# Group norm, gating and attention for 16 images on one core: the next image's statistics moved earlier, GpSimd's gating of x spread over 26 units

## The reference

```
# x: (16, 32, 32, 512) float32, that is 16 images of 1024 tokens x 512 channels
xn  = silu(group_norm(x, 32 groups) * scale + offset)     # per image, groups of 16 channels
qkv = xn @ w_qkv                                          # 512 -> 3 * 512
sim = (q * 64 ** -0.5) @ k.T                              # 8 heads of 64, 1024 x 1024 each
out = softmax(sim) @ v
y   = out @ w_out + b_out + x
```

## Time and profile before

| | us |
|---|---|
| median of 3 runs | 3637.15 |
| lowest, highest | 3636.62, 3638.37 |
| the profiled execution's own time | 3637.04 |
| its span, first to last instruction | 3635.2 |
| PE busy | 3544.2 (97%) |
| DVE busy | 3068.0 (84%) |
| ACT busy | 2698.3 (74%) |
| POOL busy | 2393.7 (66%) |

### The profile page before, as it was taken

How to read it: one execution, slowest core, us unless ns; L and a number is a source line. 1 busy time by engine, 2 the same in 40 slices (tenths; PEclk the granted TensorE clock), 3 DMA queues, 4 the chain that set the end, 5 groups by cost and what they waited for, 6 DMA issues and landing times.

```text
span 3635.2 us, 91073 instructions
## 1 busy us (share of the span) xinstructions
PE 3544.2 (97%) x31820; PEld 2068.6 (57%) x31820; DVE 3068.0 (84%) x4042; ACT 2698.3 (74%) x2818; POOL 2393.7 (66%) x2211
## 2 busy tenths in 40 slices
PE   4899999999999999999999999999999999999998
PEld 2455555555555555555555555555555555555554
DVE  6788888888888888888888888888888888888887
ACT  3587777878778787777877778777787877778776
POOL 1394775948658495684947759486584956849445
PEclk7999999999999999999999999999999999999999
DMA  2222223233132322323222232331323223222231
GB/s 90 58 53 64 70 59 93 48 85 78 36 96 48 90 64 47 88 52 82 64 67 67 59 93 47 88 75 36 96 49 88 64 48 87 52 82 64 50 85 46
DMA packets 178020, 245.87 MB, mean 68 GB/s; under 512 B 53536, under 2 KB 86304, under 8 KB 177568
## 3 DMA queue, kind: packets, MB, share of 16 engines
q1 hardware_dynamic: 177568, 239.94, 26.9%
HBM read 88.35 MB, written 33.82 MB: 34 GB/s over the span
## 4 chain that ended last, share of the span: by engine, by line
PE 76%; issue 7%; DVE 6%; POOL 4%; ACT 2%; DVEq 0%; ACTq 0%; POOLq 0%
PE SD L1099 28%; PE PV L1240 16%; PE TP L1114 10%; PE ST L1210 9%; PE ST L1211 9%; POOL Pl L621 2%; DVE mx L897 2%; DVE Pl L929 2%; PE ST L1181 1%; PE ST L1174 1%; ACT Ph L737 1%; DVE QK L826 1%; ACT QK L691 1%; DVE st L906 0%; PE SD L1163 0%
## 5 line engine op out<-in xcount | busy, mean ns | idle before, releaser
L621 POOL TENSOR_TENSOR Pl<-P,Ph 128x512 f16<-128x512 f32 x1024 | 1294.5, 1264 | 1149.0 <-ACT Ph L737 1148.8
L734 ACT ACTIVATE P<-ST,cns 128x1024 f32<-128x1024 f32 x1024 | 1142.2, 1115 | 837.2 <-PE ST L1211 781.6
L897 DVE TENSOR_REDUCE mx<-TP 128x1 f32<-128x1024 f32 x1024 | 1246.0, 1217 | 204.5 <-PE TP L1114 194.5
L737 ACT ACTIVATE Ph<-ST,cns 128x1024 f16<-128x1024 f32 x1024 | 1134.1, 1108 | 0.0
L929 DVE TENSOR_TENSOR Pl<-P,Ph 128x512 f16<-128x512 f32 x1024 | 1039.0, 1015 | 9.5 <-ACT Ph L737 4.6
L1240 PE MATMUL PV<-V,Ph 128*128 128x129 f16 (+2 forms) x10240 | 860.4, 210 | 7.0 <-DVE pv_sum L939 2.5
L1240 PEld LDWEIGHTS PV<-V,Ph 128*128 128x128 f16 x10240 | 769.8, 97 | 129.8 <-DVE pv_sum L939 9.1
L1240 PE MATMUL PV<-V,Pl 128*128 128x65 f16 x8192 | 833.0, 192 | 0.0
L1240 PEld LDWEIGHTS PV<-V,Pl 128*128 128x128 f16 x8192 | 721.4, 98 | 104.8
L1210 PE MATMUL ST<-QK 128*128 128x512 f16 x2048 | 775.5, 379 | 3.2 <-DMA QK<-shift_rows 2.2
L1211 PE MATMUL ST<-QK 128*128 128x512 f16 x2048 | 775.8, 379 | 0.0
(11 more groups left out here) (113 smaller groups left out, 2923.4 us busy)
## 6 DMA issues: line engine op xcount, KB each, us to landing
QK<-QK SPq DMA_DIRECT2D x384, 256.0 KB, 4.7
x_in<-in_x SPq DMA_DIRECT2D x61, 512.0 KB, 3.5
res<-in_x SPq DMA_DIRECT2D x120, 256.0 KB, 3.9
out<-res SPq DMA_DIRECT2D x120, 256.0 KB, 3.4
V<-V SPq DMA_DIRECT2D x16, 1040.0 KB, 7.7
QK<-shift_rows SPq DMA_DIRECT2D x256, 64.0 KB, 3.2
shift_rows<-ms SPq DMA_DIRECT2D x256, 1.0 KB, 3.0
V<-in_L_conv_w_qkv SPq DMA_DIRECT2D x4, 768.0 KB, 11.0
```

The costliest lines, as they stand in the source:

```text
L621: nc.gpsimd.tensor_tensor(Pl[:, v % 4, HALF:], P32[:, v % 2, HALF:], Ph[:, v % 4, HALF:], ALU.subtract).then_inc(lo_pool, 1)
L734: nc.scalar.activation(P32[:, v % 2, :], ST[:, slot, :], ACT.Exp, scale=cns[:, 0:1])
L737: nc.scalar.activation(Ph[:, v % 4, :], ST[:, slot, :], ACT.Exp, scale=cns[:, 0:1]).then_inc(exp_done, 1)
L897: nc.vector.reduce_max(mx[:, hh, qb:qb + 1], TP[:], AX.X).then_inc(top_drained, 1)
```

## The change

The statistics of the next image move to earlier units, and POOL's 32 gating instructions, which stood in 21 units from (1,10) on as two and one in turn, stand in 26 units from (1,4) on, one in most units and two in six. ACT's z and tanh move with them. The units in which the two statistics matmuls are made move from (0,15) to (0,13) and from (1,3) to (0,15). `LATE_BIAS_AT`, `BIAS_AT` and the turns stay where they are.

```diff
 def unit_stats(step, u, last=False):
 
-    kind = {(0, 15): "mean", (1, 3): "var"}.get((step, u))
+    kind = {(0, 13): "mean", (0, 15): "var"}.get((step, u))
     return [(kind,)] if kind and not last else []
...
-BN_AT = {(0, 5): (0, 2), (0, 7): (4, 6), (0, 11): (1, 3), (0, 13): (5, 7)}
-AGGREGATE_AT, NEWTON_AT = (0, 14), (1, 5)
-Z_AT = [(1, 8), (1, 10), (1, 13), (1, 15), (2, 2), (2, 5), (2, 7), (2, 10)]
-TANH_AT = [(1, 9), (1, 11), (1, 14), (2, 0), (2, 3), (2, 6), (2, 8), (2, 11)]
-SILU_FROM = (1, 10)
+BN_AT = {(0, 4): (0,), (0, 5): (2,), (0, 6): (4,), (0, 7): (6,), (0, 9): (1, 3), (0, 10): (5, 7)}
+AGGREGATE_AT, NEWTON_AT = (0, 11), (1, 0)
+Z_AT = [(1, 2), (1, 6), (1, 9), (1, 12), (1, 15), (2, 3), (2, 6), (2, 9)]
+TANH_AT = [(1, 3), (1, 7), (1, 10), (1, 13), (2, 0), (2, 4), (2, 7), (2, 10)]
+SILU_FROM, SILU_UNITS = (1, 4), 26
...
 def silu_ops(step, u):
 
     n = 16 * step + u - 16 * SILU_FROM[0] - SILU_FROM[1]
-    first = 3 * (n // 2) + 2 * (n % 2)
-    return [divmod(k, 4) for k in range(first, first + 2 - n % 2) if 0 <= k < 4 * PIECES]
+    if not 0 <= n < SILU_UNITS:
+        return []
+    return [divmod(k, 4) for k in range(4 * PIECES * n // SILU_UNITS, 4 * PIECES * (n + 1) // SILU_UNITS)]
```

## The result

The changed kernel takes 3682.51 us (3681.85 to 3683.05, 4 runs) against 3636.89 for the kernel before on the same chip: a ratio of 1.0125, interval 1.0107 to 1.0142, 46 us slower. The forecast was 3673, within 3645 to 3702. Lines stand one higher than before in all that follows the change (L929 is L930, and so on).

The account below looks back on a forecast made before the run. PE, busy 97% of the span, was taken as the bound, with about 2.2 us an image spent waiting on late DVE. Terms summed to +2.6 an image, times 14 +36, on 3637.0: 3673 us, range 3645 to 3702.

Parts of the forecast that it names:

- batch statistics ahead of the turn, (0,5): Two L906 instead of one ahead of L859 delay PE's turn of x: +0.60 us an image, bounds 0.5 and 0.7.
- the pair ahead of the sums of (0,10): The batch statistics pair in (0,9) delays the sums of (0,10): +0.30 us an image, 0.2 to 0.35.
- L907 pair in (0,10), L913 in (0,11), felt in (0,12): Said to stand ahead of no sums, with DVE caught up by (0,12); no cost was counted.
- mean ahead of the sums of (0,14), net: Mean's four instructions cost 0.84 in (0,14), the old pair's 0.35 goes: +0.50 us an image, bounds +0.1 and +0.7.
- (1,1): The variance's shorter block replaces the mean's in (1,0), so the maximum comes in time and this wait goes: -0.29 an image.
- POOL's queue, (1,2): Newton, then late bias L609, delay L621 to 10.3 to 10.4; PE wants it at 8.24: +2.1, bounds +0.7 and +2.7.
- (1,4): ACT's late work delays the drain of SD by 0.5, the old 0.23 wait goes: +0.27 us an image.
- gating, the 24 units from (1,10): At a lower rate L929 meets a busy POOL less often: -0.9 of 1.25 us an image.
- The blocked price: DVE and GpSimd exclude each other for whole instructions, so Newton's term is 2.1; running side by side, 0.7, total 3653.
- The pile on ACT: Exponentials of (1,2) start about 2.2 late, with z and tanh ahead of SD's drain in (1,4): 0.5, bounds 0 and 0.8.
- The clock: Rival: the wait in (1,2) drops TensorE to 1.2 GHz for 7 us an image, 3.5 more each: 3722; chance 0.03.
- a wait shorter than that leaves it: Clock falls to 1.2 GHz only after an idle window, so it was expected to stay up after the wait in (1,2).

Follow-up runs that it names:

- those that mended (0,5) or (0,12) alone: Changed kernel with first batch statistics instruction back in (0,5): 3679.23 us; separately, changed kernel with the four L913 one unit later, in (0,12): 3679.47 us.
- VectorE's part alone: Changed kernel with Newton back at (1,5) and gating tables as before, leaving batch statistics, mean and variance at their new units: 3655.93 us, ratio 1.0056.
- second placed kernel: Kernel before with batch statistics spread singly, biases at (3,1), (3,3), late biases at (1,1) to (1,4), old gating pattern two units sooner: 3636.17 us, ratio 1.0002.

## Why the prediction was right, point by point

It forecast +36 us and +46 came. The mechanism and its place were right, and the largest term to a tenth of a microsecond. That the sum came as near is in part luck: gating was taken 0.7 too well and a wait of 0.50 was overlooked, while 0.7 too much stood at (0,10) and (1,4). By its own steps, in us an image:

| step | forecast | measured |
|---|---|---|
| batch statistics ahead of the turn, (0,5) | +0.60 | +0.59 |
| the pair ahead of the sums of (0,10) | +0.30 | +0.05 |
| L907 pair in (0,10), L913 in (0,11), felt in (0,12) | 0 | +0.50 |
| mean ahead of the sums of (0,14), net | +0.50 | +0.43 |
| (1,1) | -0.29 | -0.30 |
| POOL's queue, (1,2) | +2.1 | +2.1 |
| (1,4) | +0.27 | -0.2 |
| gating, the 24 units from (1,10) | -0.9 | -0.2 |
| a fall of the clock behind (1,2), once in 14 images | 0 | +0.1 |
| image b = 14, unit (3,4) (left open) | 0 | +0.2 |

The measured column adds up to 3.3, and 3.34 is the whole. (1,2) and the 24 units are averages of the 14 images.

*The queue on POOL.* Every link is in the timelines above: the guess 2.11 into (1,0) (1.9 forecast), two small instructions held up, the bias, L622 of 1.60, and PE going on at 3.88 into (1,2), where 3.7 was the forecast. That the bias's place decides is shown by the run with it at (1,1), that Newton's place causes it at all by the run without it. The blocked price was the right one: 0.68 and 0.54 for 0.20, and L893's 1.12 for 0.17. By this the trace agrees with the exclusive lock of the Trainium skill, "SBUF — State Buffer", section "SBUF: two separate sides".

*Where a term was mis-sized.* Gating: "of the 1.25 I take -0.9" was a guess at how collisions answer to an even load. The 24 units took 82.16 and 82.04 before (b = 6 and 5), 82.33 and 81.58 after, and over all 14 images 82.11 and 81.87. The old waits did go: (2,5), (2,13) and (3,1) had 0.29, 0.13 and 0.42 an image and have nothing. But (2,2) and (2,3), which had nothing, have 0.59 and 0.17. The runs with and without the spreading differ by 1.0 us in all, their L929 takes 999 ns on average without and 998 with it, and on the kernel before spreading gained nothing. So the collisions were moved, not removed. How much the new place costs hangs on the late biases: with the first at (1,1) the 24 units take 81.43. *The pile on ACT* at (1,4), taken as 0.5, didn't come: ACT's exponentials were late by 2.2 in (1,2), but PE was as late, and both took up again together. The trace shows L735 starting 0.06 behind PE's late products.

Timeline of ACT after, the exponential of (1,2):

```profile
1511.07 1.11 ACT L735 ACTIVATE P<-ST,cns 128x1024 f32<-128x1024 f32 x1 [3.46 <-POOL Pl L622]
```

*The step that failed.* "The pair in (0,10) and the four L912 in (0,11) are ahead of no sums; DVE has caught up by (0,12)." It looked only at the sums and not at the other release that PE meets early in an even unit, the drain of SD. L868, behind the pair, meets POOL (0.87 for 0.23), the four L913 and the wait behind them follow, and L839 starts 1.68 into (0,12): 0.50. The run with L913 one unit later takes it away wholly, so L913 ahead of L839 is the cause; whether the pair has a part in it wasn't tested. With (0,10), where 0.25 too much was taken, it leaves 0.25 an image; gating, 0.7 too much gain, is partly made good by the 0.5 too much at (1,4).

*The clock.* It had 0.03 and was priced at 3.5 us an image, for every image. It does fall after the wait in (1,2), so "a wait shorter than that leaves it" doesn't hold here, but it falls in one image of 14, b = 6: (1,2) and (1,3) took 10.51 there (6.05 and 4.46, at 0.91 and 0.74 granted) and 8.83 at full clock in b = 8, so 1.7 us once. Ahead of that fall PE had been idle for 2.06 us, up to 1511.01, and busy on either side. So the forecast that it stays was nearly right for this kernel. The runs show that it hangs on more than the wait itself: with the same wait in (1,2) the clock fell in two images of 14 in the kernel with Newton at (1,0) and the old gating, and in three in those that mended (0,5) or (0,12) alone, whose images are 0.5 to 0.6 us shorter. What decides it isn't shown. All nine falls are in even images, in which PE stands 2.06 to 2.08; in the odd ones it stands about 1.9 (1.88 in b = 7), and the clock stays.

*Left open.* In the image b = 14 unit (3,4) takes 7.08 us after and 4.56 before; one row of DVE stands for it, which waited for nothing that the profile shows:

```profile
3418.90 0.75 DVE L827 SCALAR_TENSOR_TENSOR QK<-SD,sc,QK 128x512 f16<-128x512 f32 x1 [4.39 <-issue]
```

In the kernel before the same row waits too, but less:

```profile
3375.41 0.75 DVE L826 SCALAR_TENSOR_TENSOR QK<-SD,sc,QK 128x512 f16<-128x512 f32 x1 [2.67 <-issue]
```

That is 2.5 of the 46 us, in part by the clock: it fell in this unit a second time, at 3420.18 (0.88 granted over the unit), once PE had stood 1.93 for this row. The long wait comes with the new units of the two statistics matmuls: all eight kernels that have them show it, VectorE's part alone among them (4.85), and the five with the old ones, the kernel before counted, don't (the unit is at most 0.6 over a clean one). Why is open. It is in none of the other 13 images, whose steps 2 and 3 run inside the loop, while this one's stand after it.

## What to carry to other kernels

With hand-written orders and single buffers, ask of each moved instruction what release stands directly behind it on its engine, and at which point of its unit PE meets that release: a 0.6 us instruction ahead of one costs 0.6, and the same instruction a place later costs nothing. On the helper engine add up everything in the unit that receives a serial chain; the chain of 5.5 us alone cost PE 0.6, one instruction of 1.27 us more behind it made that 2.2. And an even load on an engine that holds another up is not fewer collisions: what paid (3626 against 3636) was to keep single instructions away from named releases.

## What the runs showed of the hardware

A wait of PE of about 2 us, once an image in a stream that is otherwise full, can lead to a fall of the granted clock to the lower level (1.2 GHz). It did so in some images and not in others, with the same program: after (1,2) in 1 of 14 images in the changed kernel, in 2 with Newton at (1,0) and the old gating, in 3 in the two whose images are 0.5 to 0.6 us shorter apart from it, and in no image of b = 1 to 13 of the kernels whose waits are under 1 us. Each of these cost 1.7 us. Behind the wait in (3,4) of b = 14 it fell in five kernels of the eight that have it: in the changed one after 1.93 us, and not in VectorE's part alone after 2.39. A change that removes 0.5 us of waiting an image can so gain 3 us in place of 8.

A DVE instruction on 4 elements a partition, 0.17 us alone, takes as long as the POOL instruction that lies over it: 1.12 in (1,4) of the second placed kernel. DVE's mean time for the low part says little about the kernel: it was 1015 ns before and 1024 with the gating spread, at the same time of the kernel, and 998 in the changed kernel, which is 46 us slower.
